# Gated cross-attention with a feed-forward layer: scores issued for four chunks at once, and every engine's order rewritten

## The reference, cut to what matters

```python
q = layernorm(x)                       # (16 batches, 64 channels, 512 columns)
qp = Wq @ instance_norm(q) + bq        # 64 x 512 for each batch
kp = Wk @ instance_norm(ctx) + bk
sp = Ws @ ctx + bs
attn = softmax(qp.T @ kp)              # 512 x 512 for each batch
mean    = sp @ attn.T
mean_sq = (sp * sp) @ attn.T
std = sqrt(relu(mean_sq - mean * mean))
x = x + tanh(g0) * (instance_norm(ctx) * std + mean)
x = x + tanh(g1) * (layernorm(x) @ W.T)      # W is dequantised from 4-bit integers, 512 x 512
```

## Time and profile before

| what | us |
|---|---|
| median of the runs | 191.20 |
| profiled execution, its time | 191.17 |
| profiled execution, its span | 189.4 |
| PE busy | 168.2 (89%) |
| DVE busy | 140.7 (74%) |
| POOL busy | 133.9 (71%) |
| ACT busy | 131.8 (70%) |

### The profile page before, as it was taken

The page is one execution under the profiler, slowest core; times in us unless marked ns, Lnnn a source line. Parts: engine busy times, 40 slices in busy tenths (PEclk is TensorE's granted clock), DMA queues, the critical chain, the costliest instruction groups (busy, mean ns, idle before and its releaser), DMA issues.

```text
span 189.4 us, 2916 instructions
## 1 busy us (share of the span) xinstructions
PE 168.2 (89%) x816; PEld 104.7 (55%) x816; DVE 140.7 (74%) x321; ACT 131.8 (70%) x283; POOL 133.9 (71%) x155
## 2 busy tenths in 40 slices
PE   0349699999999999989998999899979889999993
PEld 0325455665556466545654565456435444888881
DVE  3877798679976967997699769994896753585641
ACT  2365766949796879759786968697779689626210
POOL 2225578538995899679969987998979999494100
PEclk9999999999999999999999999999999999999999
DMA  6248491477068427813680470064000000021312
GB/s 188 82 96 236 110 239 44 116 172 268 2 141 262 154 49 173 294 42 88 165 294 12 105 175 0 0 157 123 3 2 0 0 0 3 5 106 55 114 55 111
DMA packets 10880, 20.09 MB, mean 106 GB/s; under 512 B 1648, under 2 KB 1776, under 8 KB 10864
## 3 DMA queue, kind: packets, MB, share of 16 engines
q1 hardware_dynamic: 10864, 19.90, 37.0%
HBM read 9.67 MB, written 2.10 MB: 62 GB/s over the span
## 4 chain that ended last, share of the span: by engine, by line
PE 64%; DVE 15%; POOL 5%; issue 4%; ACT 4%; DMA 3%; SPq 2%; DVEq 0%; POOLq 0%; ACTq 0%
PE pv_bank L364 19%; PE score_bank L340 10%; PE turn_bank L351 10%; DVE neg_max L694 4%; PE score_bank L397 4%; PE score_bank L401 4%; PE score_bank L398 4%; POOL probs L889 3%; PE proj_bank L376 3%; PE proj_bank L322 3%; DMA params_sb<-in_params 2%; POOL x_lo L882 2%; ACT probs L492 2%; PE score_bank L387 2%; SPq L249 2%
## 5 line engine op out<-in xcount | busy, mean ns | idle before, releaser
L889 POOL TENSOR_SCALAR probs<-probs,rden 128x512 f32<-128x512 f32 x64 | 55.0, 859 | 19.4 <-DVE rden L700 19.1
L492 ACT ACTIVATE probs<-score_bank,neg_max 128x512 f32<-128x512 f32 x64 | 44.5, 696 | 24.2 <-DVE neg_max L694 23.9
L364 PE MATMUL pv_bank<-probs_t,values 128*128 128x512 f32 x120 | 60.2, 604 | 0.9 <-ACT VAR L509 0.6
L694 DVE TENSOR_REDUCE neg_max<-score_bank 128x1 f32<-128x512 f32 x64 | 43.4, 680 | 18.9 <-PE score_bank L340 18.8
L351 PEld LDWEIGHTS turn_bank<-ident,probs 128*128 128x128 f32 x256 | 29.4, 141 | 27.0 <-issue 22.4
L351 PE MATMUL turn_bank<-ident,probs 128*128 128x128 f32 x256 | 37.1, 277 | 4.3 <-ACT probs_t L500 2.9
L500 ACT COPY probs_t<-turn_bank 128x512 f32<-128x512 f32 x64 | 37.9, 591 | 1.2 <-PE turn_bank L351 1.0
L364 PEld LDWEIGHTS pv_bank<-probs_t,values 128*128 128x128 f32 x120 | 19.7, 190 | 13.0 <-issue 12.5
L340 PE MATMUL score_bank<-k_hi,q_hi 64*128 64x512 f32 x32 | 16.3, 509 | 2.8 <-DVE k_lo_swapped L776 2.5
L340 PE MATMUL score_bank<-k_hi_swapped,q_hi_swapped 64*128 64x512 f32 x32 | 16.3, 509 | 0.0
L397 PE MATMUL score_bank<-w_hi,yt_hi 128*128 128x512 f32 x32 | 13.6, 424 | 0.0
(11 more groups left out here) (105 smaller groups left out, 340.2 us busy)
## 6 DMA issues: line engine op xcount, KB each, us to landing
X<-in_x SPq DMA_DIRECT2D x8, 256.0 KB, 3.0
CTX<-in_context SPq DMA_DIRECT2D x8, 256.0 KB, 3.7
q_hi_swapped<-q_hi SPq DMA_DIRECT2D x16, 128.0 KB, 2.3
q_lo_swapped<-q_lo SPq DMA_DIRECT2D x16, 128.0 KB, 2.4
ctx_now<-in_context SPq DMA_DIRECT2D x8, 256.0 KB, 2.7
sz<-in_scales_zeros SPq DMA_DIRECT2D x4, 512.0 KB, 5.1
out<-result SPq DMA_DIRECT2D x8, 256.0 KB, 2.0
k_hi_swapped<-k_hi SPq DMA_DIRECT2D x15, 128.0 KB, 2.4
```

The costliest lines, as they stand in the source:

```text
L364: mm = pe.matmul(sums_bank(t, b)[:, :], values[:, i, b, :, :].rearrange("p a c -> p (a c)"), probs_t[b][:, i, :], start=(i == 0), stop=(i ...
L492: act.activation(probs[c % SBANKS][:, :], score_bank[c % SBANKS][:, :], ACT.Exp, bias=neg_max[:, c:c + 1], accum_out=den[:, c:c + 1]).then ...
L694: dve.tensor_reduce(neg_max[:, c:c + 1], score_bank[c % SBANKS][:, :], AX_X, ALU.max, negate=True).then_inc(max_done, 1)
L889: pool.tensor_scalar(probs[c % SBANKS][:, :], probs[c % SBANKS][:, :], rden[:, c:c + 1], 1.0, ALU.mult, ALU.mult).then_inc(probs_done, 1)
```

## The change

The reference is computed by the same operations on the same engines, but for three things. The four first chunks of tile 0 are now one half-array matmul after the other (`first_scores`, twelve matmuls) instead of two paired calls, so that they need no swapped copy; the two copies on ACT and DVE that made one are gone, and the copy that tile 0 needs for b = 1 alone is still made by DMA. In `project` the product with the low part of the weights comes before the one with the low part of the activation, and only the last waits for that. k of tile 1 goes into `pv_bank` as k of tile 0 did.

Everything else is a new place in an engine's order. `scores` is issued for four chunks at once, at c = 3 (chunks 4 to 7) and c = 7 (chunks 0 to 3 of the next tile). `value_product`, `keep_values` and `square_values` are made a tile ahead, with two buffers each for `ctx_now` and `values`; k is projected two tiles ahead instead of one; `statistics` comes three tiles ahead instead of two. MEAN has two buffers instead of eight, so that `keep_sums` waits for `with_mean` and `square_mean` two tiles back. The swaps are issued for one half after the other. The four dequantisations and their splits in the last two tiles move by some c. The last `weigh` goes into `pv_bank` as the others do, where it had `proj_bank`. The order of the feed-forward part itself stays as it was. The diff below is cut to the new order (the removed orders stand in the code above); the edits for the dequantisation are left out.

```diff
+        MEAN = sb("MEAN", [P, 2, N])
...
+        ctx_now = [sb(f"ctx_now{i}", [P, N]) for i in range(2)]
...
+        values = [sb(f"values{i}", [P, JC, 2, 2, C]) for i in range(2)]
...
+            return pv_bank if which == 1 and t < 2 else proj_bank
...
                 sp.wait_ge(q_hi_done, t + 2)
+                swap(t + 1, 0, swap_q_hi)
                 sp.wait_ge(q_lo_done, t + 2)
...
+                swap(t + 1, 0, swap_q_lo)
                 sp.wait_ge(k_hi_done, t + 2)
...
+                swap(t + 1, 0, swap_k_hi)
                 sp.wait_ge(k_lo_done, t + 2)
...
+                swap(t + 1, 0, swap_k_lo)
+                swap(t + 1, 1, swap_q_hi, swap_q_lo, swap_k_hi, swap_k_lo)
+                if has_second_next(t):
+                    sp.wait_ge(s_done, t + 1)
+                    load_now(t + 2)
...
+                pe.matmul(into[:, :], w_qk_hi[:, which, :], hi[:, :], start=True, stop=False)
+                pe.matmul(into[:, :], w_qk_lo[:, which, :], hi[:, :], start=False, stop=False)
                 pe.wait_ge(lo_done, t + 1)
...
+                pe.matmul(into[:, :], w_qk_hi[:, which, :], lo[:, :], start=False, stop=True).then_inc(done, 1)
+            def first_scores(c):
+                rows = slice(0, C)
+                if c == 0:
+                    pe.wait_ge(q_lo_done, 1)
+                    pe.wait_ge(k_lo_done, 1)
+                for step, (q_part, k_part) in enumerate(((q_hi, k_hi), (q_lo, k_hi), (q_hi, k_lo))):
+                    mm = pe.matmul(score_bank[c][:, :], q_part[0][rows, P * c:P * c + P], k_part[0][rows, :],
+                                   start=(step == 0), stop=(step == 2))
+                mm.then_inc(scores_done, 1)
...
+            for c in range(SBANKS):
+                first_scores(c)
...
+                    if c == 3:
+                        scores(t, 4)
+                        scores(t, 6)
                     if c == 7 and has_next(t):
...
+                        scores(t + 1, 0)
+                        scores(t + 1, 2)
                     if not has_next(t):
                         if c == 6:
                             turn_y(0, 0)
...
+                    turn(t, c)
+                    if c == 0:
+                        if is_first(t):
+                            pe.wait_ge(q_hi_done, 2)
+                            pe.wait_ge(q_lo_done, 2)
+                            value_product(0)
+                        else:
+                            weigh(t - 1, 1, 2)
+                    if c == 1:
+                        if is_first(t):
+                            pe.wait_ge(k_lo_done, 1)
+                            project(1, 1)
+                        else:
+                            weigh(t - 1, 1, 3)
+                    if c == 3:
+                        if has_next(t):
+                            pe.wait_ge(k_hi_done, t + 2)
+                            pe.wait_ge(k_lo_done, t + 2)
+                            pe.wait_ge(s_kept, 2 * t + 2)
+                            value_product(t + 1)
+                        weigh(t, 0, 0)
+                        weigh(t, 0, 1)
+                    if c == 4:
+                        weigh(t, 0, 2)
+                    if c == 5:
+                        weigh(t, 0, 3)
+                        if has_second_next(t):
+                            pe.wait_ge(s_kept, 2 * t + 4)
+                            project(t + 2, 0)
+                    if c == 7:
+                        if has_second_next(t):
+                            pe.wait_ge(q_hi_done, t + 3)
+                            pe.wait_ge(q_lo_done, t + 3)
+                            project(t + 2, 1)
+                        if not has_next(t):
                             turn_y(1, 1)
+                        weigh(t, 1, 0)
+                        weigh(t, 1, 1)
...
+            exponentials(0, 0)
+            exponentials(0, 1)
+            keep_hi(1, 0)
...
+                    if c == 0:
+                        if has_next(t) and not is_first(t):
+                            keep_hi(t + 1, 1)
+                        exponentials(t, 2)
+                    if c == 1:
+                        keep_turned(t, 0)
+                        exponentials(t, 3)
+                        if is_first(t):
+                            keep_hi(1, 1)
+                    if c == 2:
+                        keep_turned(t, 1)
+                        if t >= 1:
+                            keep_sums(t - 1, 1)
+                    if c == 3:
+                        keep_turned(t, 2)
+                        if t >= 2:
+                            logarithm(t - 2)
+                        if not has_next(t):
+                            normalise_y(1)
+                        exponentials(t, 4)
+                        keep_turned(t, 3)
+                        exponentials(t, 5)
+                    if c == 4:
+                        if t >= 2:
+                            root(t - 2)
+                        exponentials(t, 6)
+                    if c == 5:
+                        keep_turned(t, 4)
+                        exponentials(t, 7)
+                    if c == 6:
+                        keep_turned(t, 5)
+                        keep_sums(t, 0)
+                    if c == 7:
+                        if has_second_next(t):
+                            keep_hi(t + 2, 0)
+                        keep_turned(t, 6)
+                        if has_next(t):
+                            exponentials(t + 1, 0)
+                            keep_turned(t, 7)
+                            exponentials(t + 1, 1)
...
+            statistics(1)
...
+            maximum(0, 0)
+            maximum(0, 1)
+            maximum(0, 2)
+            reciprocal(0, 0)
+            maximum(0, 3)
+            reciprocal(0, 1)
             normalise(1, 1)
+            keep_lo(1, 0)
             def body(t):
                 for c in range(CHUNKS):
...
+                    if c == 0 and not is_first(t):
+                        maximum(t, 2)
+                        maximum(t, 3)
+                        reciprocal(t, 1)
+                        if has_next(t):
+                            keep_lo(t + 1, 1)
+                    if c == 1:
+                        reciprocal(t, 2)
+                        if is_first(t):
+                            keep_values(0, 0)
+                            keep_values(0, 1)
+                    if c == 1 and t >= 4:
+                        row_statistics(t - 4)
+                    if c == 2:
+                        reciprocal(t, 3)
+                        if t >= 4:
+                            finish_statistics(t - 4)
+                        if is_first(t):
+                            statistics(2)
+                            keep_lo(1, 1)
+                        elif has_second_next(t):
+                            normalise(t + 2, 0)
+                    if c == 3:
+                        maximum(t, 4)
+                        maximum(t, 5)
+                        maximum(t, 6)
+                        reciprocal(t, 4)
+                        maximum(t, 7)
+                        reciprocal(t, 5)
+                        if is_first(t):
+                            normalise(2, 0)
+                    if c == 4:
+                        if has_next(t):
+                            keep_values(t + 1, 0)
+                            keep_values(t + 1, 1)
+                        if t >= 1:
+                            with_mean(t - 1)
+                        if has_second_next(t):
+                            normalise(t + 2, 1)
+                    if c == 5:
+                        reciprocal(t, 6)
+                        if t >= 1:
+                            square_mean(t - 1)
+                        if t >= 3:
+                            after_attention(t - 3)
+                    if c == 6:
+                        reciprocal(t, 7)
+                        if has_second_next(t + 1):
+                            statistics(t + 3)
+                        if not has_next(t):
+                            row_statistics(TILES - 4)
+                            finish_statistics(TILES - 4)
+                    if c == 7:
+                        if has_next(t):
+                            maximum(t + 1, 0)
+                        if has_second_next(t):
+                            keep_lo(t + 2, 0)
+                        if has_next(t):
+                            maximum(t + 1, 1)
+                            reciprocal(t + 1, 0)
...
+                    if c == 3 and is_first(t):
+                        inverse_deviation(2)
+                    if c == 7 and has_second_next(t + 1):
+                        inverse_deviation(t + 3)
+                    if c + 1 < CHUNKS:
+                        if not (is_first(t) and c == 0):
+                            normalise_probs(t, c + 1)
                     elif has_next(t):
...
+                        normalise_probs(t + 1, 0)
```

(17 more changed lines are left out.)

238 lines of the change are left out of this document (50 added, 188 removed).

## The result

| | before | after |
|---|---|---|
| median of the runs, us | 191.45 | 199.54 |
| range | 191.08 to 192.58 (4 runs) | 198.93 to 199.87 (4 runs) |
| span of the profiled execution | 189.4 | 198.1 |
| PE, DVE, POOL, ACT busy, us | 168.2, 140.7, 133.9, 131.8 | 171.5, 148.7, 135.6, 134.3 |

The ratio is 1.0408, 95% interval [1.0356, 1.0461]: the change makes the kernel 8.1 us slower. Slower was the likeliest case, but 194.0 was forecast and the range ended at 196.5.

What follows compares the result with a forecast made beforehand. PE sets the time from about 26 us, with GpSimd's normalisations holding its turns; 40.4 + 2 × 18.0 + 3 × 18.5 + 17.0 + 14.5 = 163.4, with 28.8 and 1.8 giving 194.0 us; 8-in-10 range 187.5 to 196.5.

Steps and rivals of the forecast that it cites:

- the double call: `scores` for four chunks at once on PE: about 1.6 us against 1.82 for two single calls, saving 0.4 a tile.
- the half tile without collisions: From the start of `scores(t,4)` to that of `scores(t+1,0)`, VectorE and GpSimd not delaying each other: 8.7 us.
- T to S: T starts `scores(t,4)`, S starts `scores(t+1,0)`; with collisions forecast at 10.0 us in tiles 3 to 5, 9.5 in tiles 1 and 2.
- the first maximum: VectorE's first maximum at the kernel's start: hardly moves from 14.89, forecast at 14.65 us behind statistics, power and normalisation.
- `turn` of chunk 6: PE idle before this turn, released by GpSimd's normalisation, 0.5 to 1.3 us once a tile.
- start, to `scores(1,4)`: Kernel's start up to tile 1's second double call: 40.4 us, gaining 0.7 at most; ends 2 better, 1.5 worse.
- to the feed-forward part: From `scores(7,4)` to the feed-forward part: 14.5 us (ends 13.5 and 15.6), normalisation 7 behind two `weights_lo` and VectorE's run.
- S to the next T: From the start of `scores(t+1,0)` to the next tile's `scores(t,4)`: 8.5 us, GpSimd deciding by 0.3 over PE's 8.2.
- as at 99.31 (+0.9): Old-profile normalisation at 99.31 us, 1.56 instead of 0.70 beside `with_mean` and `square_mean`; +0.9 was taken for normalisation 6.
- the start and more: Rival: turn 3 also waits for normalisation 3 behind `scale_context` and x's cast, 0.6 more a tile, 197 us; chance 0.07.
- PE stays the bound: Rival: VectorE and GpSimd operations fall into each other's gaps, turn 6 on time; 156.9 at feed-forward, 187.5 us; chance 0.25.
- The row of the 1.56 us normalisation: Old-profile GpSimd normalisation beside `with_mean` and `square_mean` back to back; its 0.86 priced the collisions as a middle estimate.

Runs made afterwards that it cites:

- e_early: Changed kernel with the first call of each double one issued a chunk earlier on PE, twice a tile; 197.13 us, ratio 1.0298.
- e_nolock: Changed kernel with `with_mean`, `square_mean` and `after_attention` replaced by one-input statistics of the same columns, results left out; 193.13 us, ratio 1.0061.
- e_start: Changed kernel with the old kernel's paired first scores and two copies, and `statistics(1)` ahead of `keep_lo`; 199.02 us, ratio 1.0408.
- b_start: Kernel before the change with the product of the activation's low part last in `project`, alone waiting for it; 191.09 us, ratio 0.9986.

## Why the prediction was right or wrong

**Right.** PE bound before; GpSimd's normalisations release PE after; the double call (1.6 forecast, 1.59 from 60.75 to 62.34, where single ones take 0.90 in e_early); the half tile without collisions (8.7 forecast from T to S, 8.71 in e_nolock); the first maximum (14.65 forecast, 14.74); the feed-forward part; and that slower was the likeliest side. The 17.12 of e_early, where PE is full, isn't the 16.95 of the forecast, since its calls stand singly.

**Half right.** `turn` of chunk 6 was to be the place of the wait, with 0.5 to 1.3 us. It waits 0.39 or 0.40 in each of tiles 1 to 5; the turn of chunk 2 waits 0.30 to 0.89 as well, and the projection of k up to 0.83.

**Wrong in size**, 5.9 us by the start of the feed-forward part (163.4 against 169.28):

| term | forecast | measured | off |
|---|---|---|---|
| start, to `scores(1,4)` | 40.4 | 42.54 | 2.1 |
| tiles 1 and 2, each | 18.0 | 18.21 | 0.4 in all |
| tiles 3 to 5, each | 18.5 | 18.83, 18.70, 18.65 | 0.7 in all |
| tile 6 | 17.0 | 18.65 | 1.65 |
| to the feed-forward part | 14.5 | 15.49 | 1.0 |

- *The start* (40.4). "The scores are done by 16.3 and hide behind this" nearly held: they were done by 16.8. The term failed behind it, where I took it that PE would step by 0.235 as it did in the old trace. It did so almost 8 us later than there (steps above), and `scores(0,4)` came at 24.76 instead of 21.9. That isn't all of it: e_start is fast from 20.3 and still has `scores(1,4)` at 41.37, 1.0 late, and where that lies is open.
- *T to S*, the collisions, was 0.55 too dear in tile 4 (9.45 against 10.0), and *S to the next T* 0.75 too cheap (9.25 against 8.5). The sum was near by luck. The step that failed is "normalisation 6 meets `square_mean` and `after_attention` as at 99.31 (+0.9)": it met `square_mean` alone and lost 0.43, and `after_attention` met `c_lo` behind it. The walk from S started the maximum at S + 1.05, as before; but VectorE was late from its own run, which collisions made 1.2 longer and the statistics 1.8 longer, so that it started at S + 1.67. The rival "the start and more" named this half, but a different wait in it.
- *Tile 6 and the last stretch* failed on taking tile 6 as tile 5 less its projections. The dequantisation puts more passes of two inputs into VectorE's run. VectorE and GpSimd of the changed kernel in tile 7:

```profile
160.03 1.02 DVE L747 TENSOR_TENSOR mean_sq<-MEAN 128x512 f32<-128x512 f32 x1
160.97 1.18 DVE L764 SCALAR_TENSOR_TENSOR X<-CTX,tanh_g,X 128x512 f32<-128x512 f32 x1
162.07 1.75 DVE L792 TENSOR_TENSOR w_deq<-w_deq,sz 128x512 f32<-128x512 f32 x1
```

```profile
158.87 2.74 POOL L947 TENSOR_SCALAR probs<-probs,rden 128x512 f32<-128x512 f32 x2
161.58 1.70 POOL L959 TENSOR_TENSOR w_lo<-w_deq,w_hi 128x512 fp32r<-128x512 f32 x1
```

```profile
164.81 0.66 PE L362 MATMUL turn_bank<-ident,probs 128*128 128x128 f32 x4 [1.86 <-POOL probs L947]
```

Two normalisations take 2.74 instead of 1.35, and PE then waits 1.86. With the three passes of one input, tile 6 takes 17.43 and the last stretch 14.49 (e_nolock), near the 17.0 and 14.5 of the forecast: 2.2 of the 2.65 that these terms were off are more collisions than I had counted.

The rival "PE stays the bound" asked what the order does when nothing collides; e_nolock shows it, 5.8 us above that rival at the feed-forward part (162.67 against 156.9): 2.5 the start, 1.8 in tiles 1 to 5, 1.4 behind them. So even without the collisions of these three passes the order wouldn't have beaten the old one. The row of the 1.56 us normalisation, with two passes of VectorE in a row beside it, had a price of 0.86 that no single meeting in the middle tiles reached (0.43 each), and I counted too few meetings: I looked for it in one place per tile and should have walked the whole list of VectorE's two-input passes against GpSimd's.

One line of the working is wrong as written: a double call has four steps of 0.235 behind the first of 0.33, not five. Four, with the tail of 0.32, make the 1.6 that the sum uses.

## What to carry to other kernels

Before packing passes of VectorE into a run, list which of them collide with GpSimd (here those with two SBUF inputs, and some casts), and walk each against what GpSimd does at that moment; a price of 0.4 us a meeting, on both engines, made 6.4 of the 8.1 us that this reorder lost. An idle gap of VectorE in which GpSimd is idle or near the end of its pass is the place for such a pass: moving one pass of 0.73 us into such a gap won 1.3%, where the whole reorder, mended, won nothing. When a wait is taken away, look for the chain behind it: b_start removed PE's wait for `x_lo` and gained nothing. And a run that ends with the pass that starts the next chain must be walked to its end, since every delay in it arrives there at once.
